# One tile body instead of three for TensorE, SyncE and GpSimd, and one instead of two for ScalarE and VectorE, in the expert loop of an attention and mixture-of-experts kernel

## The reference

```python
x = L0_attn_hidden_states                       # [4, 1024, 256]
x = x + layernorm(attn(layernorm(x), ...))      # per batch; rope, exp sums, small MLP
x = x + layernorm(ffn(layernorm(x), ...))

def ffn(x, gate_w, gate_b, w1, b1, w2, b2):     # 8 experts, D = 256, F = 1024
    flat = x.reshape(-1, 256)                   # 4096 rows
    logits = flat @ gate_w + gate_b
    topv, topi = top_k(logits, 2)
    topw = softmax(topv)
    routing = zeros.at[rows, topi].set(topw)
    for e in range(8):
        h = gelu(flat @ w1[e] + b1[e])
        acc += (h @ w2[e] + b2[e]) * routing[:, e]
```

## Time and profile before

| | |
|---|---|
| median of three runs | 690.49 us |
| the profiled execution | 689.87 us |
| its span (first to last instruction) | 688.0 us |
| TensorE (PE) busy | 559.7 us, 81% |
| VectorE (DVE) busy | 486.0 us, 71% |
| ScalarE (ACT) busy | 290.4 us, 42% |
| GpSimd (POOL) busy | 185.8 us, 27% |
| mean granted TensorE clock | 0.904 |
| instructions in the trace | 14407 |

### The profile page before, as it was taken

One profiled execution on the slowest core, in us unless ns is written; L12 is line 12 of the kernel. 1 busy time (PEld: TensorE's weight loads), 2 busy tenths in 40 slices (PEclk: granted clock), 3 DMA queues, 4 the chain that ended last, 5 costly groups with the idle time before them and its releaser, 6 DMA issues.

```text
span 688.0 us, 14407 instructions
## 1 busy us (share of the span) xinstructions
PE 559.7 (81%) x4170; PEld 509.3 (74%) x4175; DVE 486.0 (71%) x1579; ACT 290.4 (42%) x669; POOL 185.8 (27%) x153
## 2 busy tenths in 40 slices
PE   2768787686496899999999987999999959999700
PEld 1636363452476899999999976999999959999700
DVE  4968888697746676666666667767576768697547
ACT  3364656676162533333333443323233714553250
POOL 2000170533615541323232310222232203132300
PEclk9968879798598999999999998999999979999955
DMA  8910020640315732323232462323232643523286
GB/s 223 379 42 0 9 101 15 230 154 31 108 17 200 205 72 37 54 38 53 39 54 38 123 165 69 46 47 46 46 46 50 174 130 46 153 48 53 47 288 214
DMA packets 51865, 66.91 MB, mean 97 GB/s; under 512 B 4870, under 2 KB 45292, under 8 KB 51692
## 3 DMA queue, kind: packets, MB, share of 16 engines
q1 hardware_dynamic: 37804, 47.87, 21.8%
q0 software_dynamic: 14016, 18.56, 15.5%
HBM read 38.26 MB, written 28.74 MB: 97 GB/s over the span
## 4 chain that ended last, share of the span: by engine, by line
PE 66%; DVE 17%; issue 8%; ACT 5%; DMA 2%; DVEq 1%; ACTq 0%; SPq 0%; POOL 0%; POOLq 0%
PE pY L1374 26%; PE pL L1362 25%; PE pP L755 3%; PE pS L733 2%; PE pS L677 2%; PE pX L1347 2%; ACT xn L515 2%; DVE z L1527 2%; PE pP L660 2%; DVE w_lo L178 1%; PE pS L719 1%; DVE mstats L953 1%; DVE x_all L948 1%; PE pT L645 1%; PE pT L747 1%
## 5 line engine op out<-in xcount | busy, mean ns | idle before, releaser
L1295 ACT ACTIVATE h<-pL,b_now 128x256 f32<-128x256 f32 x272 | 114.1, 471 | 252.0 <-PE pL L1362 251.1
L466 POOL DMA_INDIRECT sum_y<-y,dest x72 | 117.6, 1633 | 317.2 <-DVE y L1426 280.4
L1374 PE MATMUL pY<-w_hi,h_lo 128*128 128x256 f32 x544 | 156.4, 287 | 14.1 <-DVE h_lo L1399 14.1
L1362 PE MATMUL pL<-xeT_hi,w_lo 128*128 128x256 f32 x544 | 153.5, 282 | 9.0 <-issue 6.5
L1374 PE MATMUL pY<-w_hi,h_hi 128*128 128x256 f32 x544 | 153.1, 281 | 0.0
L1374 PE MATMUL pY<-w_lo,h_hi 128*128 128x256 f32 x544 | 152.9, 281 | 0.0
L1362 PE MATMUL pL<-xeT_lo,w_hi 128*128 128x256 f32 x544 | 152.7, 281 | 0.0
L1362 PE MATMUL pL<-xeT_hi,w_hi 128*128 128x256 f32 x544 | 152.4, 280 | 0.0
L1374 PEld LDWEIGHTS pY<-w_hi,h_lo 128*128 128x128 f32 x544 | 104.6, 192 | 14.8 <-DVE h_lo L1399 14.8
L1362 PEld LDWEIGHTS pL<-xeT_hi,w_lo 128*128 128x128 f32 x544 | 103.8, 191 | 10.6 <-issue 7.7
L1374 PEld LDWEIGHTS pY<-w_hi,h_hi 128*128 128x128 f32 x544 | 104.8, 193 | 0.0
(11 more groups left out here) (223 smaller groups left out, 810.0 us busy)
## 6 DMA issues: line engine op xcount, KB each, us to landing
w_stage<-w SPq DMA_DIRECT2D x16, 1024.0 KB, 8.9
xt<-sorted_x SPq DMA_DIRECT2D x38, 260.0 KB, 2.7
sum_y<-fill SPq DMA_DIRECT2D x1, 4352.0 KB, 20.4
w_stage<-sum_y SPq DMA_DIRECT2D x8, 512.0 KB, 6.9
out<-z SPq DMA_DIRECT2D x8, 512.0 KB, 3.1
x_all<-x SPq DMA_DIRECT2D x3, 1024.0 KB, 8.5
sorted_x<-fill SPq DMA_DIRECT2D x8, 260.0 KB, 2.6
sum_y<-y,dest POOLq DMA_INDIRECT x72, 3.9
```

The costliest lines, as they stand in the source:

```text
L466: pool.indirect_dma_start(out=sum_y, out_offset=bass.IndirectOffsetOnAxis(ap=dest[:, i:i + 1], axis=0), in_=y[:, i, :], in_offset=None, co ...
L1295: a = act.activation(h[:, c, :], pL[:, bk, i * TM:(i + 1) * TM], ACT.Gelu, bias=b1_now[par][:, c:c + 1])
L1362: mm = pe.matmul(pL[:, bk, i * TM:(i + 1) * TM], w[:, 0, col], x[:, k, :], start=(k == 0 and w is lo), stop=(k == KC - 1 and x is xeT_lo))
L1374: mm = pe.matmul(pY[:, i, 0:D], s[:, c, rows], w[:, 1, c * D:(c + 1) * D], start=(c == 0 and s is h_lo), stop=(c == FC - 1 and w is lo))
```

## The change

`over_tiles` gets a second form, taken when `first` is None: two nested loops of four rounds with an `If` in each run all tiles of an expert from one body. TensorE, SyncE and GpSimd use it. For ScalarE and VectorE `first` stays, and the tiles behind it are run by the same two nested loops, from one body.

```diff
                 if start:
                     start(e, pair, par, base)
+                if first is None:
+                    with eng.Fori(0, TPE // 4) as u:
+                        with eng.If(n > 4 * u):
+                            with eng.Fori(0, 4) as v:
+                                with eng.If(n > 4 * u + v):
+                                    tile(e, who, par, base + 4 * u + v)
+                    return
                 with eng.If(n >= 1):
                     first(e, who, pair, par, base)
                     with eng.If(n >= 2):
-                        rest = n + 3
-                        with eng.Fori(0, 3) as v:
-                            with eng.If((rest & 3) > v):
-                                tile(e, who, par, base + 1 + v)
-                        with eng.If(n >= 5):
-                            fours = base + 1 + (rest & 3)
-                            with eng.Fori(0, 3) as u:
-                                with eng.If((rest >> 2) > u + 1):
-                                    with eng.Fori(0, 4) as v:
-                                        tile(e, who, par, fours + 4 * u + v)
+                        with eng.Fori(0, TPE // 4) as u:
+                            four = 4 * u + 1
+                            with eng.If(n > four):
+                                with eng.Fori(0, 4) as v:
+                                    with eng.If(n > four + v):
+                                        tile(e, who, par, base + four + v)
...
-            def first(e, who, pair, par, g):
-                tile(e, who, par, g)
-
-            over_tiles(sp, None, start, first, None, tile)
+            over_tiles(sp, None, start, None, None, tile)
...
-            over_tiles(pool, None, None, first, None, tile)
+            over_tiles(pool, None, None, None, None, tile)
...
-            over_tiles(pe, None, start, first, None, tile)
+            over_tiles(pe, None, start, None, None, tile)
```

## The result

The changed kernel takes **709.19 us** (median of 4 runs, 704.65 to 710.75); the kernel before takes 689.43 beside it. The ratio is **1.025, 95% interval 1.022 to 1.029**. Slower was the likeliest outcome of the prediction, but the time lies outside its range (686.5 to 702.5), 14 us above the 695 forecast. The profiled execution took 709.84 us with a span of 708.1.

The account below looks back on a forecast made before the run. TensorE's matmuls were taken to bound the expert phase, any idle there paid in full; -19.9 - 2.0 + 18.8 + 8.1 = +5.0 us on 689.87 gave 695 us, own range 691 to 699, wider range 686.5 to 702.5.

Parts of the forecast that it names:

- VectorE's two holes gone, minus 19.9 us: Third, fifth and seventh experts' first tiles: VectorE's shorter pair loop ends its instruction-fetch holes, 55.8 to 35.9 us.
- 1 us twice: Behind the first and third expert: cost of VectorE's empty rounds if a later TensorE no longer covered them.
- this sum holds, because TensorE will come later too: Third, fifth and seventh experts' first tiles: the 19.9 us saving stays even if a hole's first part (3.4 us) remains.
- Empty rounds, plus 18.8: TensorE at experts' edges: failed rounds of 0.8 us each raise idle time from 5.5 to 24.3 us.
- The clock, plus 8.1: TensorE behind the idles at experts' edges: the granted clock halves for a while, costing 8.1 us.
- The step from a loop of three to loops of four, minus 2.0: TensorE in the first and third expert: the issue step between loops goes, saving 2.0 us.
- The other engines, zero: Empty rounds on ScalarE, VectorE, SyncE and GpSimd are covered and cost zero; bound 2 us.
- A (holes stay, 702.5): VectorE's pair loop of some 236 instructions still has both parts of the holes; 702.5 us, chance 0.17.
- B (the clock holds): TensorE's granted clock does not fall behind idles of 3 to 5 us; 686.8 us, chance 0.15.
- C (cheap rounds): TensorE's empty rounds cost less: sum zero at 0.62 us a round, 678 us at 0.4; chance 0.08.
- D (hidden edges): VectorE or weights late at the experts' edges, so gain and loss both shrink; about 690 us, chance 0.06.
- from the sixth expert's start to the seventh's: Sign in the changed profile: some 16.5 us, against 12.0 from the fourth's start to the fifth's before.

Follow-up runs that it names:

- the padded kernel: Changed kernel with 40 never-run waits in each copy of VectorE's branch for experts without tiles; 1.024 of the kernel before.
- the kernel with TensorE alone in three bodies: Changed kernel with TensorE alone put back to its three bodies, as in the kernel before; 707.13 us, 0.984 of the kernel before.
- the filling transposes: Changed kernel with four transposes into an unused bank in each of TensorE's empty rounds; 1.021 of the kernel before.
- the loop that ends at n: Changed kernel with one body looping to the tile count on TensorE, GpSimd, ScalarE and VectorE; 0.972, later 0.968 (668.46 us) of the kernel before.

## Why the prediction was wrong

**The step that failed is "VectorE's two holes gone, minus 19.9 us".** The holes went as said, and the mechanism is shown by the padded kernel: with a longer loop VectorE fetches code again at the jump back. The size is wrong twice. First, alone the part is worth 10.4 us by the medians (11.5 with SyncE and GpSimd changed too). The three first tiles go from 55.79 to 40.63, 15.2 us and not 19.9. One of them, the third expert's, takes 14.45 us, because TensorE's far branch still lets the clock fall ahead of it: the granted clock is 0.50 for its first 5.8 us. In the kernel with TensorE alone in three bodies the clock is 1.00 there, this tile takes 11.66 and the three together 37.02, near the 35.9 of the prediction. And 3.8 us come back in the one-tile experts (39.60 to 43.40), where TensorE now waits for VectorE, late by its own empty rounds. The prediction had this price, "1 us twice", for the case that TensorE's lateness is gone. Second, and more, beside TensorE's empty rounds the part is worth between nothing (by the ratios) and 6 us (by the stage). With the holes still there, TensorE's lateness alone brings its waits for `h_lo` from 14.1 down to 2.7 us. The kernel with TensorE alone changed has the holes and the ratio 1.023; the changed kernel has none and 1.025, 1.013 and 1.023; the padded one has them again and 1.024. The prediction used the cover of a late TensorE for the first part of a hole alone ("this sum holds, because TensorE will come later too") and then took the rest of the hole as a saving in full, though its own table had TensorE 5 us late at just these two places.

**Empty rounds, plus 18.8.** The idle times in the order of the experts were forecast as 1.5, 5.05, 2.25, 5.0, 3.1, 4.5, 2.9 and are 1.93, 6.03, 2.83, 6.00, 3.95, 5.35, 3.83; by the starts their sum is 31.1, not 24.3. An inner round is 0.74 us (0.8 forecast), but an outer one 0.93, and the entry into the two loops, 0.88 us in the row above, for each of seven experts, was not counted. The size is off by 6.8 us.

**The clock, plus 8.1.** Half of the time at 0.50 behind the seven edges is 16.9 us in the first profile and 14.9 in the second. The clock also fell behind the short idle times, where 0 to 0.8 us had been put, and behind the others it stayed low for 5.0 to 5.8 us, not for 4.2. This cost is on the path. A tile at full clock takes 11.34 us; the first tiles of the changed kernel, 14.25, 14.22 and 14.43, are that plus half of their slow stretches (2.7, 2.7 and 2.9) and 0.2, and with the filling transposes, where the stretch is 3.4 us, they are 13.2 to 13.4. In the loop that ends at n they take 12.6 to 13.2 at full clock for another reason: TensorE, no longer late, waits up to 1.27 us for VectorE's `h_lo`. From ScalarE and VectorE alone to the whole change the time rises by 26.5 us (679.71 to 706.21), by 22.6 in the stage, where the terms of the prediction give 18.8 + 8.1 - 2.0 = 24.9. In the stage TensorE's idle time at the edges grows by 24.0 us and half the slow time by 8.6, while its waits for `h_lo` (4.7) are gone and the "rest" is 3.9 shorter: 24.0, of which 22.6 are measured. So idle and clock cost more than forecast, and the waits that a late TensorE is spared, which the prediction did not count, made up for it.

**The step from a loop of three to loops of four, minus 2.0.** The 0.88 us of issue are gone from the chain of the first expert, and the two steps where they stood (first and third expert) fall from 12.38 and 12.27 us to 11.56 each, 1.5 us in sum: right, if a little large. The "rest" of the stage falls by 1.9, but it differs by 2.8 between the changed kernel's own profiles.

**The other engines, zero.** Right for the whole change, since SyncE and GpSimd add nothing to the ratio of VectorE's part (0.984 with and without them). Wrong by themselves: 0.9% off the time, through an order of transfers that the prediction took for harmless because SyncE "waits some 2 us for the weight split anyway". Its six empty rounds take 4.7 us (404.39 to 409.13), not 1.8, and outlast that wait: the weights went out at 410.60 instead of 407.02.

**The sum.** By the medians of one occasion VectorE and ScalarE give -10.4 and TensorE (with SyncE and GpSimd) +26.5 on top, together +16.1, where the prediction has -19.9 + 24.9 = +5.0. Of the 11 us between them 9.5 are the holes' term. That the other 1.6 are so few is in part luck, since idle times forecast too short and a saving left out cancel there. The first measurement shows +19.8; of the 4 us more, 3.3 are in the stage (425.95 against 422.61), 1.5 of them in the first one-tile step (19.70 against 18.23). There the granted clock fell behind the idle time in the one profile (0.53) and not in the other (1.00); why is open. So is the start of the first expert, which lies between 226.6 and 229.7 us in the kernels measured outside the two slower occasions and doesn't follow any one part.

**The rivals.** A (holes stay, 702.5) did not happen, and its price of 7.6 us is too high: with the holes put back, a little shorter, the ratio is unchanged and the stage 1.2 us longer, and with TensorE alone changed, where they have their full length, TensorE waits 2.7 us for them in all. The rule it named, from the Trainium skill, "Runtime: NRT & Kernel Launch", section "Instruction fetch mechanics", that a taken branch out of the two resident pages stalls, agrees with the trace in part: there are holes with some 310 and 314 instructions in the loop, none with 236. But the same section has 256 instructions in a page, so that 310 would fit into two; whether the loop lies across three, or fetching ahead drops its head, no run here shows. B (the clock holds) and C (cheap rounds) did not happen. D (hidden edges) was right about the mechanism, cover, and wrong about its balance: it was mostly the gain that was covered. The rule on branches, the Trainium skill, "Advanced Engine Details and Errata", section "Control Flow Timing", some 108 ns for a compare-and-branch, differs from TensorE's rows, 208 to 221 ns taken and 76 to 83 not; the measurement decides. One sign of the prediction shows the miss of idle and clock at once: from the sixth expert's start to the seventh's it was to be some 16.5 us and is 19.7.

## What to carry to other kernels

Two stalls of different engines at the same place are not two terms of a sum: price each with the other in place and with it gone. Here the holes were worth 10 us alone, and at most 6 beside TensorE's lateness. Before a loop gets rounds that do nothing, count its control instructions on the engine that sets the time, entry and exit too; a loop that ends at the count itself costs none of them and here beat both kernels by 3 and 5%. Where one engine jumps far back in its code, look for what has just been put into the DMA queues.

## What the runs showed of the hardware

Code is fetched in packets that the trace lists in an instruction queue, and such a packet can be late behind data: 8 KB that take 0.3 us came 4 us late when 2 MB of weights had gone out ahead of them, and a delay of 2 us on another engine's issue took 0.8% off the kernel. Length alone makes the holes: some 40 instructions in each of two branches that never run were enough.

The clock's fall does not follow the idle time alone. Behind 1.93 us it fell in the changed kernel's first profile; behind 1.91 us ahead of the same expert it did not in the second (below). Nor did it behind 3.15 us ahead of the third expert in the kernel with TensorE alone in three bodies (granted 1.00 from 433.90 to 448.76 us), where 3.12 us at the same place lowered it with ScalarE and VectorE alone changed.
```profile
415.10:417.02 1.92, 0.01 (x2) 0.01 (x1) 1.61 (x8) 0.00 (x0) 0.35 (x1) 1.00 0.24 82
417.02:420.42 3.40, 3.40 (x28) 3.40 (x29) 0.52 (x1) 1.07 (x3) 2.81 (x2) 1.00 0.79 279
```
Idle times of 0.3 to 1.1 us did not lower it at the edges of the loop that ends at n, in either of its two profiles.
